# Low one-hots of a recommender's attention made by ScalarE out of PSUM, not by a VectorE compare

## The reference, cut to what is computed

```python
item_emb = concatenate([table_i1[item[:, 0]], table_i2[item[:, 1]], table_i3[item[:, 2]]], axis=1)
ub = concatenate([table_i1[rec_his[:, :, 0]], table_i2[rec_his[:, :, 1]], table_i3[rec_his[:, :, 2]]], axis=2)
mask = rec_his[:, :, 0] == 0
att_in = concatenate([q, ub, q - ub, q * ub], axis=-1)
h = att_in @ w_att1.T + b_att1
score = where(mask, 0.0, (h @ w_att2.T + b_att2)[..., 0])
browse = einsum('bl,ble->be', score, ub)
feat = concatenate([item_emb, browse, user_emb], axis=-1)
# then two dense layers with _dice, and a sigmoid
```

## Time and profile before

| | before |
|---|---|
| median of 3 runs | 1508.28 us |
| span of the profiled execution | 1506.3 us |
| DVE busy | 1405.9 us, 93% |
| PE busy | 1299.2 us, 86% |
| POOL busy | 1188.4 us, 79% |
| ACT busy | 758.1 us, 50% |
| granted PE clock, 60 to 1440 us | 0.98 |
| DMA share, 60 to 1440 us | 0.66 |

### The profile page before, as it was taken

One profiled execution on the slowest core, in us unless ns is written; L12 is line 12 of the kernel. 1 busy time (PEld: TensorE's weight loads), 2 busy tenths in 40 slices (PEclk: granted clock), 3 DMA queues, 4 the chain that ended last, 5 costly groups with the idle time before them and its releaser, 6 DMA issues.

```text
span 1506.3 us, 66273 instructions
## 1 busy us (share of the span) xinstructions
PE 1299.2 (86%) x27007; PEld 1186.0 (79%) x27007; DVE 1405.9 (93%) x1397; ACT 758.1 (50%) x1729; POOL 1188.4 (79%) x1671
## 2 busy tenths in 40 slices
PE   5688989889898988889898998989899898988864
PEld 4577878888887988788788888878888887888761
DVE  6699999999999999899999999999999999999945
ACT  5554455555445555454555554454555545452217
POOL 3588788888888888788888888888888888888830
PEclk8899999999999999999999999999999999999966
DMA  3566676666667666666766666666676666565820
GB/s 51 111 137 127 127 143 133 141 144 141 124 137 143 130 146 140 127 133 133 143 131 142 146 141 134 130 137 132 143 143 140 141 132 138 131 149 133 153 54 1
DMA packets 517508, 194.38 MB, mean 129 GB/s; under 512 B 485445, under 2 KB 493237, under 8 KB 517245
## 3 DMA queue, kind: packets, MB, share of 16 engines
q1 hardware_dynamic: 499654, 162.61, 53.5%
q10 hardware_dynamic: 15448, 26.51, 6.7%
q0 software_dynamic: 2144, 1.36, 0.8%
HBM read 8.45 MB, written 1.44 MB: 7 GB/s over the span
## 4 chain that ended last, share of the span: by engine, by line
POOL 72%; issue 15%; PE 3%; DVE 3%; POOLq 3%; ACT 2%; DMA 1%; ACTq 1%; SPq 0%; DVEq 0%
POOL score L439 24%; POOL score_r L448 14%; POOL score L444 11%; POOL parts L449 9%; POOL parts L452 6%; POOL item_rows L417 4%; POOL parts L445 3%; POOL user_rows L425 2%; DVE score_j L1026 1%; DVE onehot_lo L1012 1%; ACT scores_b L775 1%; PE sel L727 1%; DMA hiT<-onehot_hi 1%; POOLq L437 1%; POOLq L443 1%
## 5 line engine op out<-in xcount | busy, mean ns | idle before, releaser
L560 PE MATMUL wsum_ps<-scaled_lo,onehot_hi 100*128 100x75 bf16 x12288 | 535.0, 201 | 81.5 <-DVE scaled_lo L1038 80.2
L543 PEld LDWEIGHTS sel<-scoretab,hiT 128*128 128x128 bf16 x12288 | 495.8, 99 | 121.6 <-DMA hiT<-onehot_hi 59.2
L543 PE MATMUL sel<-scoretab,hiT 128*128 128x75 bf16 x12288 | 534.5, 201 | 63.1 <-DMA hiT<-onehot_hi 43.9
L1038 DVE TENSOR_TENSOR scaled_lo<-onehot_lo,parts 100x3744 bf16<-100x3744 bf16 x256 | 539.0, 2105 | 34.4 <-POOL parts L452 26.4
L560 PEld LDWEIGHTS wsum_ps<-scaled_lo,onehot_hi 100*128 100x128 bf16 x12288 | 486.1, 99 | 106.3 <-DVE scaled_lo L1038 101.7
L439 POOL TENSOR_TENSOR score<-score_j 100x16 f32<-100x16 f32 x256 | 386.6, 1510 | 156.6 <-DVE score_j L1026 155.7
L768 ACT ACTIVATE wsum_ring<-wsum_ps 128x300 f32<-128x300 f32 x512 | 215.5, 421 | 525.7 <-PE wsum_ps L560 497.2
L1026 DVE TENSOR_REDUCE score_j<-sel 100x24 f32<-100x600 f32 x512 | 395.5, 772 | 21.0 <-PE sel L543 21.0
L994 DVE TENSOR_TENSOR onehot_hi<-digits,iota_hi 100x1920 bf16<-100x1920 bf16 x256 | 296.1, 1157 | 3.4 <-PE wsum_ps L560 3.3
L775 ACT ACTIVATE scores_b<-acc 128x512 bf16<-128x512 f32 (+1 forms) x318 | 255.4, 803 | 50.0 <-issue 22.7
L448 POOL TENSOR_TENSOR score_r<-score,parts 100x16 f32<-100x16 f32 x256 | 207.3, 810 | 20.0
(11 more groups left out here) (168 smaller groups left out, 724.0 us busy)
## 6 DMA issues: line engine op xcount, KB each, us to landing
scoretab<-scores_b SPq DMA_DIRECT2D x384, 93.8 KB
weightsum<-wsum_ring ACTq DMA_DIRECT2D x128, 125.0 KB
weightsum<-wsum_ring ACTq DMA_DIRECT2D x64, 150.0 KB
raw<-in_r_rec_his_dram SPq DMA_DIRECT2D x32, 150.0 KB
hiT<-onehot_hi SPq DMA_TRANSPOSE x256, 3.8
x_rows<-x_tile SPq DMA_DIRECT2D x14, 100.0 KB
scores_b<-x_rows SPq DMA_DIRECT2D x1, 1400.0 KB
item_rows<-in_L_rec_table_i_dram,ids_now POOLq DMA_INDIRECT x51
```

The costliest lines, as they stand in the source:

```text
L543: mm = pe.matmul(sel[:, 2 * (s % 2) + q, (c % 4) * W:(c % 4 + 1) * W] .rearrange("p (j v) -> p j v", j=NF), hiT[0:HJ, s // 2 % 4, g * POSP ...
L560: mm = pe.matmul(wsum_ps[:, s % 2, b * W:(b + 1) * W].rearrange("p (j v) -> p j v", j=NF), hi_columns(ring_slot(n), g), scaled_lo[:, n % 2 ...
L1038: ins = dve.tensor_tensor(scaled_lo[:, n % 2, :, :, :].rearrange("p q i (u d) -> p (q i) u d", d=2), onehot_lo[:, n % 2, :, :, :].rearrang ...
```

## The change

`onehot_low` leaves DVE's program and stands at the head of each slot of ACT's. ACT waits on `score_ready` for pick(s) and reads the same sums of `sel` once more, as Relu(1 + sel * 2/FAR): at the digit's column that is 1, elsewhere 1 - 2d² or less, so 0. It is done in two halves, one for each slot, each 100 x 600 elements in fp32 from PSUM, written in bf16. As the sums have 75 columns, `onehot_lo` and `scaled_lo` have 76 (U = W + 1, the last column zeroed once) in place of 78. PE's read_scores(s) now waits for ACT's onehot_low(s-2) too; scale(n) waits for both halves. The ACT copy of the low digits waits on `lo_rows_ready` instead of `lo_ready`.

```diff
-    HJ, U, W = HB + NF * HI, NF * LP, NF * LO
+    HJ, W = HB + NF * HI, NF * LO
+    U = W + 1
@@
-        onehot_lo = sb("onehot_lo", [POS, 2, PER, NF, LP], BF16)
+        onehot_lo = sb("onehot_lo", [POS, 2, PER, U], BF16)
+        one = sb("one", [POS, 1])
@@ read_scores
                     pe.wait_ge(score_ready, k - 1)
+                    pe.wait_ge(lo_ready, k - 1)
@@ act
+            def onehot_low(t, s):
+
+                k = t * SLOTS + s
+                n, g0 = s // 2, (s % 2) * 8
+                act.wait_ge(score_ready, k + 1)
+                if s % 2 == 0 and not (isinstance(k, int) and k < 4):
+                    act.wait_ge(scaled_ready, t * STEPS + n - 1)
+                act.activation(onehot_lo[:, n % 2, g0:g0 + 8, 0:W].rearrange("p (q c) u -> p q c u", q=2),
+                               sel[0:POS, 2 * (s % 2):2 * (s % 2) + 2, 0:4 * W].rearrange("p q (c u) -> p q c u", u=W),
+                               ACT.Relu, bias=one[:, :], scale=2.0 / FAR).then_inc(lo_ready, 1)
@@
             def slot(t, s, odd, last=False):
                 here = tasks_of(t)
+                onehot_low(t, s)
@@ dve
-            def onehot_low(t, n):
...
-                dve.tensor_tensor(onehot_lo[:, n % 2, :, :, :].rearrange("p q j (v d) -> p (q j) v d", d=2),
...
-                                  ALU.is_equal).then_inc(lo_ready, 1)
@@ scale
-                dve.wait_ge(lo_ready, k + 1)
+                dve.wait_ge(lo_ready, 2 * k + 2)
@@ step
-                onehot_low(t, n)
                 pick(t, 2 * n + 1)
```

More of the change, by code:

```diff
@@ L174, in build @@
         lo_ready = sem("lo_ready")
+        lo_rim_zero = sem("lo_rim_zero")
         hiT_in = [sem(f"hiT_in{i}") for i in range(4)]
@@ L561, in add_scores @@
                                        hi_columns(ring_slot(n), g),
-                                       scaled_lo[:, n % 2, g, i % 3, :].rearrange("p (j v) -> p j v", j=NF)[:, :, 0:LO],
+                                       scaled_lo[:, n % 2, g, i % 3, 0:W].rearrange("p (j v) -> p j v", j=NF),
                                        start=(i == 0 and b == 0), stop=(i == 5), skip_group_check=True)
@@ L803, in task @@
                         else:
-                            act.wait_ge(lo_ready, (t - 1) * STEPS + 8 * hb + 8)
+                            act.wait_ge(lo_rows_ready, (t - 1) * STEPS + 8 * hb + 8)
                     src = (misc_b if kind == 1 else misc)[0:POS, 0:2 * NF * HALF]
@@ L921, in slot @@
                     split_copy(r, stage, SPLIT_DONE * (t + 1) + (3 * r + stage + 1), 1 - odd)
-            act.wait_ge(bias_ready, 4)
+            act.wait_ge(bias_ready, 5)
             scale_raw(0, 0)
@@ L1039, in scale @@
                     scaled_lo[:, n % 2, :, :, :].rearrange("p q i (u d) -> p (q i) u d", d=2),
-                    onehot_lo[:, n % 2, :, :, :].rearrange("p q j v -> p q (j v)").unsqueeze(2)
+                    onehot_lo[:, n % 2, :, :].unsqueeze(2)
                     .to_broadcast([POS, PER, 3, U]).rearrange("p q i (u d) -> p q i u d", d=2),
@@ L1076, in _ @@
             dve.memset(offset[:, :], -float(MID) / LO).then_inc(bias_ready, 1)
+            dve.memset(one[:, :], 1.0).then_inc(bias_ready, 1)
             dve.memset(w2col[:, :], 0.0).then_inc(dve_tail_pre, 1)
@@ L1096, in _ @@
             dve.memset(hiT[:, :, PER * POSP:], 0.0).then_inc(dve_tail_pre, 1)
+            dve.memset(onehot_lo[:, :, :, W:U], 0.0).then_inc(lo_rim_zero, 1)
+            dve.wait_ge(lo_rim_zero, 1)
             dve.wait_ge(rim_zero, 1)
```

## The result

The changed kernel takes 1548.82 us (median of 4 runs, 1541.08 to 1560.77) where the kernel before takes 1506.8 us in the same comparison (median of 4 too): a ratio of 1.0288, 95% interval 1.0236 to 1.0341. It is slower by 2.9%. The forecast was 1431 us, 5% faster; rival 2 had 1540 us. The profiled span is 1547.2 us.

The account below looks back on a forecast made before the run. DVE (93% busy) was the first suspect, with PE or ACT full in some stretches; taking the largest need per stretch saved 4.8 us a tile, 77 us in 16: 1506.3 + 2.0 - 77 = 1431 us, range 1362 to 1492 us.

Parts of the forecast that it names:

- rival 2: ACT's loop ends last, averaging 5.75 us in slots with a piece: 1540 us, chance 0.09; 0.11 that it just eats the gain.
- What the change takes away: On DVE, compare gone (0.75 us) and scale 0.05 us shorter: 0.80 us a step, 205 us over 16 tiles, ceiling 1303 us.
- POOL's chain: Scale waits on POOL's parts: 0.19 us of the 0.80 come back, so a DVE step is 4.61 us; more with gathers.
- The price on ACT: Each Relu takes 0.76 us, two a step; with overlap 0.65 us a slot, 21 us a tile more on ACT.
- hidden under the 4.61 us step just so: ACT and PE's two-slot loop with a piece takes 4.66 us in an even slot and was taken not to lengthen DVE's step.
- 674 to 690 and 728 to 738: Two stretches of the tile, one with gathers: forecast 14.2 us for 16.0 and 9.2 us for 10.0.
- 708 to 728: Stretch with digits, collected sums and score pieces: ACT needs 21.8 us but can catch up, so 19.6 us for 20.0.
- PE's full stretch: Stretch 690 to 708 with the products of `finish`: PE is full, yet some modelled time can go, 17.4 us for 18.0.
- DVE alone: Tile's last stretch, 738 to 747.5: only DVE's need counts, 8.4 us for 9.5.
- Rival 3: Transposition: lo_rows ends 0.65 us later, lengthening each of PE's 58 waits for `hiT`; 38 us come back, 1469 us, chance 0.10.
- Rival 1: DVE and POOL stay the bound, ACT's and PE's full stretches smoothed by the two buffers: 1366 us, chance 0.15.
- The tile's sum: Six stretches of one tile added up: 80.0 us for 84.8, 4.8 us a tile less, 77 us in 16 tiles.

Follow-up runs that it names:

- the lagging kernel: Changed kernel with the Relu of the slot before, waiting for pick(s-1), at the head of each ACT slot: 1420.81 us, ratio 0.9473.
- compare and Relu both: Kernel before, DVE compare kept, with the same Relu added at the head of ACT's slots into a scratch tile, PE waiting for it: 1601.16 us, ratio 1.0642.

## Why the prediction was wrong, point by point

- **What the change takes away: right.** 0.05 us off scale (2.105 to 2.056 us), the compare gone.
- **POOL's chain: about right.** At a tile's end in the lagging kernel, where DVE sets the pace, DVE's timeline gives 4.48 and 4.65 us for a step (4.61 forecast). In the first, scale starts 0.69 us behind the pick and waits for nothing; in the second 0.88 us behind it, which is the forecast wait of 0.19 us. So the wait is there in one step of the two:

```profile
694.97 0.78 DVE L1028 TENSOR_REDUCE score_j<-sel 100x24 f32<-100x600 f32 x1
...
696.79 0.77 DVE L1028 TENSOR_REDUCE score_j<-sel 100x24 f32<-100x600 f32 x1
697.48 2.04 DVE L1040 TENSOR_TENSOR scaled_lo<-onehot_lo,parts 100x3648 bf16<-100x3648 bf16 x1
...
699.45 0.77 DVE L1028 TENSOR_REDUCE score_j<-sel 100x24 f32<-100x600 f32 x1
...
701.20 0.77 DVE L1028 TENSOR_REDUCE score_j<-sel 100x24 f32<-100x600 f32 x1
702.08 2.10 DVE L1040 TENSOR_TENSOR scaled_lo<-onehot_lo,parts 100x3648 bf16<-100x3648 bf16 x1
...
704.10 0.77 DVE L1028 TENSOR_REDUCE score_j<-sel 100x24 f32<-100x600 f32 x1
```

- **The price on ACT: right.** 0.76 us forecast, 0.759 measured (the estimate by the Trainium skill, ScalarE: Activation LUTs, What ACT_TABLE_LOAD costs, was 0.78; the trace agrees within 3%). ACT's busy time grew by 0.58 us for each Relu, 0.65 forecast. The rule of the Trainium skill (ScalarE: Activation LUTs, Rules for kernel authors), that relu belongs on VectorE, isn't what decided: in another place the same Relu makes the kernel 5% faster.
- **The step that failed is "hidden under the 4.61 us step just so".** I had the loop pick, Relu, sums, lo_rows, piece, PE's piece, read, and priced it at 4.66 us, 0.5 more with a DMA issue, 0.8 more with digits. The prices were not too low: both loops shown have a DMA issue, which makes 5.16 us for 4.88 measured, and with digits 5.96 for 5.58. What was wrong is the assumption that they would be hidden. They are above the step of 4.61 us, and in the stretches 674 to 690 and 728 to 738 I put nothing for them at all; for 708 to 728 I argued that ACT could run behind and catch up. The runs show the loop on the path: with the same work lagging by a slot, slots 4 to 9 take 1.05 us less, 18 to 23 1.81 us and 24 to 27 0.92 us. Slots 4 to 9 were forecast about 1.8 us shorter than before and came out 0.23 us shorter; 24 to 27 were forecast about 0.8 us shorter and came out 0.28 us longer. A loop that has no cover left must be summed slot by slot, its additions too; busy shares don't bound it. The 497.2 us that ACT waited before were read as room. Most of it is still there (405.9 us for the pick), but it now stands ahead of everything in the slot, so nothing queued behind can use it.
- **PE's full stretch was given a gain that it doesn't have.** The forecast made the stretch 690 to 708 0.6 us shorter. In slots 10 to 17 PE is busy throughout, and every kernel without the compare takes 0.2 to 0.6 us more there than the one before. Why PE needs a little more time for the same matmuls is open.
- **"DVE alone" at the edge failed too.** Slots 28 to 31 were to be 1.1 us shorter; they came out 0.99 us longer, by the long wait on `hiT`. Without that wait the step holds: the lagging kernel is 1.5 us shorter there. Rival 3 had the resource and the wrong size and cause: not 0.65 us on each of 58 waits, but one of 3.2 to 6.8 us at 14 of 15 edges, beside the copies of sums, and the half clock behind it.
- **Not seen at all:** onehot_high waits 56.8 us for PE's sums (3.3 us before): it writes into a ring from which `add_scores` must have read first. It is there in all the faster kernels too (43.7 us in the lagging one), so it isn't what made this one slow, and with compare and Relu both (40.4 us), so it doesn't need a faster DVE.
- **Rivals.** Rival 2's time, 1540 us, was the nearest, and its loop the right one; but it asked for a Relu of 0.96 us, and the loss came with 0.76. That its time came so near is in part luck: it put the loss into the slots with a piece, and of the 2.35 us that a tile is longer than before, 1.86 lie at the edge. Rival 1 (1366 us) can't be: even with no Relu the time is 1409.5 us, and PE is busy all through slots 10 to 17.
- **The tile's sum was right for another kernel.** 4.8 us a tile forecast; the lagging kernel gains 5.3 (87.69 to 82.36). The terms of work were fit for the sum, with misses that cancel: 1.8 us forecast and 1.3 measured in slots 4 to 9, 1.1 and 1.5 in 28 to 31. The order in ACT's queue wasn't weighed.

Open: why a transposition issued together with a copy of sums lands so late, what makes slots 0 to 3 longer, and how much of the 75 us more at half clock is cause and not effect.

## What to carry to other kernels

When an instruction moves to a less busy engine, ask first what it will wait for, and put it where that is already done: an in-order engine passes the wait to everything queued behind. An engine's share of busy time says if the work fits, not if its place does; here one place was 2.9% slower, another 5.3% faster, with the same work. If one edge of the loop has a burst of DMA, look there before counting a light stretch as gain.

## What the runs showed of the hardware

Behind 15 of the 17 long waits PE came back at a granted clock of 0.50: the 24 matmuls took 1.70 us instead of 1.01 to 1.02; behind the one shown this lasted about 5 us. With one such wait a tile, the time at the lower level rose from about 55 to about 130 us. The transpositions of the changed kernel land after 3.6 us in the median; the one shown kept PE waiting until 8.7 us after its issue, where copies of sums and score placements were under way beside it. Where such a copy was issued 0 to 0.4 us behind the transposition, PE waited over 3 us at 39 of 41 edges, and at 7 of 79 otherwise.
